# Turning the rows of the routed experts as two planes of 2-byte words instead of one plane of fp32

## What is computed

```python
x = x + gnn0(layernorm(x))            # two SAGE convolutions
x = x + routed_experts(layernorm(x))  # this case: the second line
x = x + gnn1(layernorm(x))            # two SAGE convolutions
x = x + gated_experts(layernorm(x))   # shared MLP and four small experts
```

```python
gate_scores = x @ Wg + bg
_, idx = jax.lax.top_k(gate_scores, 2)
mask = one_hot(idx, 8).sum(axis=-2)
h = gelu(einsum('td,edh->teh', x, W1) + b1)      # exact gelu, 256 -> 512
y = einsum('teh,ehd->ted', h, W2) + b2           # 512 -> 256
out = einsum('ted,te->td', y, mask)
```

## Time and profile before

| | |
|---|---|
| median of 3 runs | 1183.03 us (1182.34 to 1183.16) |
| profiled execution, first to last instruction (its own time) | 1182.9 us |
| mean granted TensorE clock, 1 being 2.4 GHz | 0.990 |
| TensorE busy with matmuls | 1135.1 us, 96% |
| VectorE, ScalarE, GpSimd busy | 48%, 31%, 14% |
| DMA | 118.16 MB, 100 GB/s on average |
| the stage in question, tiles 1 to 27 | 461.7 to 661.2 us |

### The profile page before, as it was taken

The page is one execution under the profiler, slowest core; times in us unless marked ns, Lnnn a source line. Parts: engine busy times, 40 slices in busy tenths (PEclk is TensorE's granted clock), DMA queues, the critical chain, the costliest instruction groups (busy, mean ns, idle before and its releaser), DMA issues. The chain is left out here.

```text
span 1182.9 us, 22185 instructions
## 1 busy us (share of the span) xinstructions
PE 1135.1 (96%) x8024; PEld 853.5 (72%) x8024; DVE 563.3 (48%) x1532; ACT 361.8 (31%) x697; POOL 168.6 (14%) x160
## 2 busy tenths in 40 slices
PE   5989999999999997999999699999999999999998
PEld 4667777776668886888888577555566688866765
DVE  8888888834447677111111363000044355248654
ACT  5764554422211102333333333100022201044333
POOL 3300000000000456444445300000000000001000
PEclk9999999999999998999999799999999999999999
DMA  6610000047532446456664521120066445135101
GB/s 194 211 44 13 25 25 12 25 127 180 160 102 91 134 131 186 67 116 145 121 151 76 124 89 45 49 83 32 17 160 186 136 131 162 58 98 179 44 22 42
DMA packets 134097, 118.16 MB, mean 100 GB/s; under 512 B 23030, under 2 KB 122105, under 8 KB 134016
## 3 DMA queue, kind: packets, MB, share of 16 engines
q1 hardware_dynamic: 103392, 77.67, 22.8%
q0 software_dynamic: 12448, 18.95, 8.1%
q10 hardware_dynamic: 18176, 20.45, 5.1%
HBM read 67.34 MB, written 49.29 MB: 99 GB/s over the span
## 5 line engine op out<-in xcount | busy, mean ns | idle before, releaser
L1364 PE MATMUL b_pa<-adj,l_parts 128*128 (+2 forms) x980 | 141.7, 296 | 0.4 <-ACT adj L1295 0.4
L1364 PEld LDWEIGHTS b_pa<-adj,l_parts 128*128 128x128 f16 x980 | 91.2, 97 | 29.5 <-issue 0.5
L2907 POOL DMA_INDIRECT x<-ring,l_row_i x56 | 87.4, 1561 | 113.1 <-DMA x<-ring,l_row_i 75.5
L2714 PE MATMUL l_sum<-l_parts,ring 128*128 128x256 f32 x448 | 101.6, 380 | 0.2 <-ACT ring L2811 0.2
L1605 DVE SCALAR_TENSOR_TENSOR l_parts<-dense,scale,l_parts 128x256 f16<-128x256 f32 x48 | 23.2, 483 | 158.2 <-ACT l_parts L1596 158.2
L1572 PE MATMUL dense<-room,ring 128*128 128x512 f32 x200 | 93.9, 593 | 0.2 <-ACT ring L1553 0.2
L2714 PEld LDWEIGHTS l_sum<-l_parts,ring 128*128 128x128 f32 x448 | 83.0, 190 | 10.9 <-ACT ring L2811 0.4
L2290 PE MATMUL l_sum<-l_parts,adj 128*128 128x256 f16 x735 | 82.9, 273 | 1.2 <-DVE rows L2018 1.2
L2290 PE MATMUL l1b_sum<-l_parts,adj 128*128 128x256 f16 x735 | 82.9, 273 | 0.9 <-DVE rows L2018 0.9
L2290 PEld LDWEIGHTS l_sum<-l_parts,adj 128*128 128x128 f16 x735 | 71.2, 98 | 10.7 <-issue 2.7
L2290 PEld LDWEIGHTS l1b_sum<-l_parts,adj 128*128 128x128 f16 x735 | 71.4, 98 | 10.4 <-issue 2.4
(11 more groups left out here) (471 smaller groups left out, 1879.5 us busy)
## 6 DMA issues: line engine op xcount, KB each, us to landing
ring<-sums_and_zt SPq DMA_DIRECT2D x50, 256.0 KB, 3.4
l_expert_xr<-slots_in SPq DMA_DIRECT2D x28, 257.0 KB
l_parts<-in_L_ffn_W SPq DMA_DIRECT2D x12, 512.0 KB, 5.2
pre<-room ACTq DMA_DIRECT2D x34, 128.0 KB, 2.1
sums_and_zt<-ring SPq DMA_DIRECT2D x10, 320.0 KB, 2.3
ring<-inv SPq DMA_DIRECT2D x50, 64.0 KB, 4.0
sums_and_zt<-room ACTq DMA_DIRECT2D x5, 640.0 KB, 3.6
adj<-xt SPq DMA_DIRECT2D x5, 640.0 KB, 4.5
```

The lines of the kernel that those rows point to most:

```text
L1364: ins = nc.tensor.matmul(pa[f][:, 0:size], parts[:, k, a, f * P:(f + 1) * P], adj[:, k, ds(r * BW, size)], start=k == 0 and a == 0, stop=k ...
L2714: ins = nc.tensor.matmul(to[t], h[:, n, t * P:(t + 1) * P], w2[:, u, n, :], start=i == 0, stop=i == HB - 1)
L2907: pool.indirect_dma_start(out=g["x1"], in_=y[:, half, t, :], in_offset=None, compute_op=ALU.add, out_offset=bass.IndirectOffsetOnAxis(ap=i ...
```

## The change

The rows are turned as 2-byte words. A fp32 word is looked at as two fp16 words (`a` = 0 and 1); for each of the two, TensorE makes four transposes of 128x128 fp16 whose stationary operand is every second 2-byte word of the rows, with an fp16 identity. The two planes stand side by side in the same PSUM bank, 512 words of 2 bytes each. ScalarE then makes two copies of 128x512, one for each plane, from 2-byte words in PSUM to every second 2-byte word of `l_expert_xt`, so that both together are the fp32 values bit for bit; the second of the two signals `xt_ready`. The fp16 identity is made once by ScalarE from the fp32 one, in `second_conv` behind `take_flat(0)`, in the buffer `third`; tile 0's turn waits for it (`ident_ready`). All else is as before.

```diff
 first_tile = {"xt": pr.sb("expert_xt", [P, KD, ST], F32), "xr": pr.sb("expert_xr", [P, ST // P, DW], F32),
+              "ident": third.bitcast(F16)[:, 0:P], ...
@@ in second_conv, ScalarE
     take_flat(0)
+    if routing:
+        follow["scalar_ident"](act)
@@ in experts
-    px, px_first = (banks[n][:, :].rearrange("p (k n) -> p k n", k=KD) for n in (0, 3))
+    px, px_first = (banks[n][:, :].bitcast(F16).rearrange("p (a k n) -> p a k n", a=2, k=KD) for n in (0, 3))
+    ident = tile["ident"]
@@ turn_rows
-        for k in range(KD):
-            for t in range(NT):
-                ins = nc.tensor.transpose(to[:, k, t * P:(t + 1) * P], xr[:, t, k * P:(k + 1) * P], g["ident"][:, :])
+        for a in range(2):
+            for k in range(KD):
+                for t in range(NT):
+                    words = xr[:, t, k * P:(k + 1) * P].bitcast(F16).rearrange("p (d a) -> p d a", a=2)[:, :, a]
+                    ins = nc.tensor.transpose(to[:, a, k, t * P:(t + 1) * P], words, ident)
         ins.then_inc(s["turned"], 1)
@@ start_early
         if what == "rows":
+            pe.wait_ge(s["ident_ready"], 1)
             turn_rows(pe, 0, px_first)
@@ take_rows
-        nc.scalar.activation(xt, turned, ACT.Identity).then_inc(s["xt_ready"], 1)
+        for a in range(2):
+            ins = nc.scalar.activation(xt.bitcast(U16).rearrange("p k (n a) -> p k n a", a=2)[:, :, :, a], turned[:, a].bitcast(U16), ACT.Copy)
+        ins.then_inc(s["xt_ready"], 1)
+    def scalar_ident(act):
+        nc.scalar.activation(ident, g["ident"][:, :], ACT.Copy).then_inc(s["ident_ready"], 1)
```

More of the change, by code:

```diff
@@ L11 @@
 from concourse import mybir
-F32, F16, BF16, I32 = mybir.dt.float32, mybir.dt.float16, mybir.dt.bfloat16, mybir.dt.int32
+F32, F16, BF16, I32, U16 = mybir.dt.float32, mybir.dt.float16, mybir.dt.bfloat16, mybir.dt.int32, mybir.dt.uint16
 ALU = mybir.AluOpType
@@ L1818, in second_conv @@
             first_tile = {"xt": pr.sb("expert_xt", [P, KD, ST], F32), "xr": pr.sb("expert_xr", [P, ST // P, DW], F32),
-                          "ids_now": row_i[:, 0:2 * (ST // P)].rearrange("p (a t) -> p a t", a=2)}
+                          "ident": third.bitcast(F16)[:, 0:P], "ids_now": row_i[:, 0:2 * (ST // P)].rearrange("p (a t) -> p a t", a=2)}
             weights = expert_weights(parts, pr.sb("expert_w1", [P, KD, H0], F32), pr.sb("expert_b1", [P, 2, HB], F32))
@@ L2600, in experts @@
     whole, whole1, halves = [py[:, 0, :], py[:, 1, :]], [py1[:, 0, :], py1[:, 1, :]], [py[:, 0, :], py1[:, 0, :]]
-    s = {n: pr.sem("e_" + n) for n in ("w_in0", "w_in1", "w_free0", "w_free1", "rows_in", "turned", "xt_ready", "h_mm",
+    s = {n: pr.sem("e_" + n) for n in ("w_in0", "w_in1", "w_free0", "w_free1", "rows_in", "turned", "xt_ready", "ident_ready", "h_mm",
                                        "h_done", "y_mm", "y_done", "ids_ready", "ids_now", "adding", "added", "all_added", "first_in", "all1_set", "squared", "totalled", "rooted",
@@ L2924, in gpsimd @@
         pool.sem_inc(s["all_added"], 1)
-    return {"sync_early": sync_early, "scalar_early": scalar_early, "sync": sync, "start": start_early, "tensor": tensor, "scalar": scalar, "vector": vector, "gpsimd": gpsimd}
+    return {"sync_early": sync_early, "scalar_ident": scalar_ident, "scalar_early": scalar_early, "sync": sync, "start": start_early, "tensor": tensor, "scalar": scalar, "vector": vector, "gpsimd": gpsimd}
 def last_experts(nc, io, g, rows_from, out, final, space, ring, dense_bank):
```

## The result

| | |
|---|---|
| changed kernel | 1187.78 us median of 5 runs (1186.47 to 1190.05) |
| before, beside it | 1182.34 us median of 5 runs (1179.96 to 1183.16) |
| ratio | 1.0047, 95% interval 1.0033 to 1.0062 |
| profiled execution of the changed kernel | span 1185.0 us, own time 1186.47 us, clock 0.992 |

The change costs 0.47%, slower by more than the 0.2% bound. The forecast was 1184.9 us, or +1.85, within 0.2%. The time lies 2.9 us above that and inside the stated range by 0.2 us.

A forecast was written before the change was run, and what follows sets the result against it. TensorE was taken to bound tiles 1 to 27 (199.22 of 199.50 us busy). Turn 1.65 plus changes of expert 0.2 gave 1.85 us, so 1184.9 us (+0.16%), range 1183.0 to 1188.0.

The forecast's parts named there:

- rival 4: Row load late at the seven changes of expert, at most 0.43 us each, 3.0 in all: 1187.9 us; chance 0.05.
- The term for the turn: TensorE's eight transposes plus an exposed fp32 load: 497 ns against 436, 61 ns more, 1.65 us over 27 turns.
- The term for the changes of expert: TensorE waits for ScalarE's later copies at seven first tiles of an expert: 0.09, 0.08, 0.02, 0.01 and nothing, together 0.2 us.
- The copies' price: ScalarE's two copies last 598 ns each, the next starting 0.49 us after the first, so `xt_ready` comes 0.49 us later.
- The upper end taken, 687 ns: Dearest price for each ScalarE copy, from a 128x512 copy to fp16 with a scale operand: 0.09 us more each.
- The slack: Time from copy's end to first product's load at seven changes of expert: 0.34 to 0.67 us, less 0.11 for release.
- TensorE shows no wait for a DMA in the whole stage: SyncE's row load, 0.49 us later behind `ids_ready`, was taken as hidden, at no cost, at changes of expert too.
- Rival 1: Strided load shows at 60 ns, or copies take the upper end, or both: 1185.6 to 1186.5 us; chance 0.22.
- Tile 0 and the identity: Tile 0's later copy costs 0.03 us beyond TensorE's idle time; ScalarE's identity copy, some 0.3 us, costs nothing.
- All behind is shifted only: Sign of being right: the stage from 461.7 is 1.9 us longer and everything behind it merely moves later.
- The base of the sum: Added 1.85 us to the profiled span of 1182.9, giving 1184.7, then 0.1 for the median: 1184.9 us.

The follow-up runs named there:

- the runs of the turn alone: Changed kernel with one copy per tile instead of two (tile 0 keeps both), run twice: 1185.11 and 1184.88 us, ratios 1.0014 and 1.0016 against before.
- fp32_twice: Kernel before, with an extra packed ScalarE copy to fp16 (598 ns) ahead of the real one: 1183.81 us, ratio 1.0008 against before.
- full_third: Changed kernel, unaltered, run again as a mark in a later comparison: 1187.21 us, ratio 1.0033 against before.
- lean_again: Changed kernel without ScalarE's unused read of the tile count at a change of expert, second run: 1186.80 us, ratio 1.0026 against before.
- the experiment that was to separate the weights' share: Expert weights issued earlier on SyncE: changed kernel also without ScalarE's tile-count read, 1190.44 us, 1.0056; kernel before, 1193.11 us, 1.0096.
- lean_registers: Changed kernel without ScalarE's unused read of the tile count at a change of expert, first run: 1186.67 us, ratio 1.0031 against before.
- full_again: Changed kernel, unaltered, repeated as the mark of its comparison: 1186.85 us, ratio 1.0038 against before.

## Why the prediction was partly right

The time lies within the range, but not by the forecast's mechanism alone. The range reached up to 1188.0 for the sake of rival 4, all seven row loads late, which no trace shows; that the measured 1187.78 is next to that rival's 1187.9 is luck. The term for the turn came as forecast. The term for the changes of expert was 0.2 us and measured 2.6.

**TensorE's part: right.** 61 ns a tile were forecast and 63 came. The term has both pieces: starts 56 ns apart (eight matmuls in 0.61 us, 219 ns each: (610 - 219) / 7 = 56), so the strided load of weights is hidden, and the second product's first matmul 435 ns long, against the 379 of its line, because a fp32 load doesn't fit behind 56 ns. The piece shows in that matmul's length; its start is at 0.45 us after the turn's, not at 0.50. The Trainium skill (TensorE: Matmul & The Clock Gate, "Back-to-back issue gap") has 81 ns a pair at 128 columns; the trace has 56, and the runs of the turn alone (+1.5 and +1.9 us) leave no room for it.

**The copies' price: the step that was mis-sized.** "Each lasts 598 ns, but the next starts 0.49 us after the first". They last 741 and start 0.60 apart, so the delay is 0.74 us and not 0.49. The upper end taken, 687 ns, was still too low. With 0.74 in the prediction's own formula (delay less slack less 0.06, for slacks of 0.34 to 0.67) the seven changes give 0.34 + 0.33 + 0.27 + 0.26 + 0.15 + 0.10 + 0.01 = 1.5 us instead of 0.2. At tile 14, where ScalarE's register reads took 0.08 longer as well, the formula gives 0.42, which is what the trace has. The Trainium skill (ScalarE: Activation LUTs, "What ACT_TABLE_LOAD costs") puts an ACTIVATE without pointer operands at 186 ns and 0.833 ns an element, fp32 and bf16 alike; worked out from that figure, 512 elements are an estimated 612 ns. Of the packed 2-byte copy that holds (598), of the one written at a stride it doesn't (744).

**The slack was read from one execution.** The formula's 1.5 us is still short of the trace's 2.6. Some 0.2 of the rest is the late weights of tile 19. The other 0.9 is ScalarE's copy, which comes at another time behind the register reads than in the trace of before (single reads at the changes took 0.27 to 0.60 us there and 0.27 to 0.54 in the changed kernel's trace, the long ones at other tiles): at tile 11 it ends 4.30 us after the turn's start, where 3.15 before and 0.74 of delay make 3.89; at tile 7, where a read of 0.60 us became one of 0.28, it ends 0.3 earlier than such a sum. fp32_twice shows the same with the delay as priced: 0.8 us for 0.45.

**"TensorE shows no wait for a DMA in the whole stage", so a later load is hidden: a step that failed too.** The absence of a wait doesn't say how much room there is. The weights' load was not priced at all, though it stands in the queue that was forecast to move. In the first trace of the changed kernel this is worth 0.2 us, in that of full_third some 1.2 us (rows at tiles 7 and 14, weights at tile 9), in that of lean_again all 2.4 us. Rival 4 named this kind of loss, up to 3.0 us, by the rows alone; in lean_again it is the weights more than the rows.

**Rival 1** ("just over the bound", 1185.6 to 1186.5) has the right mechanism, the copies' upper end, and fell 1.3 us short by its size; its other half, a strided load that shows at 60 ns, did not come.

**Tile 0 and the identity.** The identity cost 0.30 us beside idle time, as said. The copies of tile 0 end 0.7 us later, and no run isolates what that is worth.

**"All behind is shifted only": not seen in the traces, because they scatter.** Tile 27's second product ends 5.1 us later than before, 1.7 of it there already at tile 2's turn (470.89 against 469.22); the clock had fallen inside tile 1 (below). The next stage's transposes start 2.6 us later, the span is 2.1 longer. What ends the stage differs from execution to execution. VectorE's first work of the next stage waited for a load in lean_again (first row) and for its own last addition in the changed kernel (second row):

```profile
DVE l_st L198 <- DMA room<-x: 3.7, 2, 3.2
```

```profile
DVE l_st L198 <- DVE ring L2869: 0.3, 1, 0.3
```

The thirteen traces compared have 7.7 or 9.9 to 11.5 us from the end of the last second product to the first transpose of the next stage (line 228), with no relation to the edits: the changed kernel has 7.7 in one trace and 10.9 in another. So the sum is made from stage parts and timed runs, and not from one span against another.

**The base of the sum.** The prediction put the median 0.1 above the profiled span. In the changed kernel the profiled execution's own time is 1.5 above its span, so the span of before, 1182.9, was not its own time. The step started from the median in effect, so the forecast stands as it was; the reason given for it was wrong.

**Still open.** Removing the register read took 0.8 and 1.0 us off the mean of the timed runs, which is not clear of their scatter either time, and left 1.5 to 1.9 us above the turn alone. That late loads make up that rest was argued from one of two traces; the other shows no waits. Differences of two such means are good to 1.4 us or so, and the experiment that was to separate the weights' share moved too much else. No kernel tried is quicker than before.

## What to carry to other kernels

Before delaying a signal, follow everything that is issued behind it, in every queue, and measure each one's distance from issue, or end, to use; a wait that doesn't appear may be 0.3 us away. Check a named wait in the timeline: what came last may be another. Where several producers arrive within a microsecond of one another, removing the last of them buys only the distance to the next, and slacks of one trace are samples of something that varies. Halving a TensorE pass and doubling its count gained nothing here, and it exposed the next stationary operand's load.

## What the hardware showed that was not expected

- A ScalarE copy of 128x512 2-byte words from PSUM takes 598 ns packed and 744 ns when written to every second word; at fp32, 256 wide, the stride costs 16 ns (400 against 384).
- The granted clock drops near the start of the stage in most traces, but not at the same place. In the changed kernel it fell inside tile 1's second product, where TensorE has no idle time to hide it: 0.81 from 461.70 to 470.89, with that product 5.38 us long in place of 3.67. Before, it had fallen in the stretch ahead, where TensorE waits for VectorE (0.81 from 444.00 to 461.70). Stretches of the changed kernel, then of before:

```profile
444.00:461.70 17.70, 10.34 (x89) 7.39 (x85) 14.29 (x77) 4.24 (x11) 11.13 (x12) 1.00 0.74 231
461.70:470.89 9.19, 8.67 (x32) 7.23 (x33) 8.27 (x50) 4.15 (x10) 7.36 (x7) 0.81 0.35 107
```

```profile
444.00:461.70 17.70, 11.94 (x75) 8.18 (x75) 13.31 (x73) 4.41 (x12) 10.96 (x12) 0.81 0.72 228
461.70:470.89 9.19, 9.12 (x48) 8.12 (x49) 7.79 (x52) 3.87 (x10) 7.36 (x7) 1.00 0.38 114
```

  Of the repeats, lean_registers has it there too (0.81) and full_again and lean_again don't (1.00), so it comes with the execution and not with the change.
